# An attention and FFN kernel: T banks taken in turn by all that ScalarE empties, two y banks, projections and the split of batch 0 moved

## What is computed

```python
Q, K, V = (proj(Wq), proj(Wk), proj(Wv))            # einsum('oc,bct->bto', W, x), 16 heads of 8
att = einsum('bhqd,bhkd->bhqk', Q, K) / sqrt(8) + b[0]
att = att * m + (1.0 - m) * NEG_INF                 # m: mask of the keys
y = einsum('bhqk,bhkd->bhqd', softmax(att), V)      # then back to (B, C, T)
h = silu(bit_linear(y, w_gate)) * bit_linear(y, w_up)   # 256 -> 1024
h = rms_norm(h, ln_weight)
out = x + bit_linear(h, w_down)                     # 1024 -> 256
# bit_linear: x rounded to 8 bit by its row maximum, w rounded to -1, 0, 1 by its mean |w|
```

## Time and profile before

| | us |
|---|---|
| median of 3 runs | 220.28 |
| lowest and highest run | 220.03, 223.39 |
| the profiled execution's own time | 221.76 |
| its span in the profile | 220.0 |
| mean granted TensorE clock in it | 0.937 of full speed |

### The profile page before, as it was taken

How to read it: one execution, slowest core, us unless ns; L and a number is a source line. 1 busy time by engine, 2 the same in 40 slices (tenths; PEclk the granted TensorE clock), 3 DMA queues, 4 the chain that set the end, 5 groups by cost and what they waited for, 6 DMA issues and landing times.

```text
span 220.0 us, 4111 instructions
## 1 busy us (share of the span) xinstructions
PE 155.7 (71%) x1378; PEld 69.2 (31%) x1378; DVE 140.9 (64%) x228; ACT 134.3 (61%) x264; POOL 106.5 (48%) x196
## 2 busy tenths in 40 slices
PE   3326859979697697687586587969378758688454
PEld 2222424324333333232242242433122321244243
DVE  5956484865575567557657646646554297699882
ACT  2011115878479588768657636636378757899852
POOL 8329956352317308207302102080873089999960
PEclk9999999997889999999999969587889996999999
DMA  3256712452612461511311210000000000000012
GB/s 123 62 146 211 162 38 55 102 211 73 181 69 53 101 202 46 169 41 36 82 42 45 70 44 2 5 0 2 0 2 3 0 4 3 0 24 24 27 48 72
DMA packets 20068, 14.19 MB, mean 65 GB/s; under 512 B 2112, under 2 KB 19144, under 8 KB 20048
## 3 DMA queue, kind: packets, MB, share of 16 engines
q1 hardware_dynamic: 19184, 13.54, 21.8%
q10 hardware_dynamic: 864, 0.39, 0.7%
HBM read 6.17 MB, written 1.07 MB: 33 GB/s over the span
## 4 chain that ended last, share of the span: by engine, by line
PE 37%; POOL 22%; DVE 14%; issue 13%; ACT 7%; DMA 3%; ACTq 2%; POOLq 1%; SPq 1%; DVEq 0%
PE y_ps L902 14%; PE s_ps L864 8%; DVE maxes L728 8%; POOL hw L418 6%; PE t_ps L881 4%; POOL h_rs L429 3%; PE misc L849 2%; ACT probs L457 2%; PE misc L923 2%; DMA q_st<-nm_rows 2%; ACTq L227 2%; POOL y_q L357 2%; PE misc L840 2%; ACT y_raw L526 2%; DVE y_n L684 1%
## 5 line engine op out<-in xcount | busy, mean ns | idle before, releaser
L728 DVE TENSOR_REDUCE maxes<-s_ps 128x4 f32<-128x1024 f32 x64 | 77.7, 1224 | 53.5 <-PE s_ps L864 53.2
L457 ACT ACTIVATE probs<-t_ps 128x512 f32<-128x512 f32 x128 | 71.2, 595 | 29.9 <-PE t_ps L881 27.0
L864 PE MATMUL s_ps<-k_st,q_st 64*128 64x256 bf16 x256 | 48.3, 315 | 5.7 <-DVE maxes L728 4.0
L902 PE MATMUL y_ps<-probs,v_pad 128*32 128x256 f32 x512 | 46.7, 430 | 5.3 <-ACT y_raw L526 5.2
L881 PE MATMUL t_ps<-q_st,k_st 64*128 64x256 bf16 x256 | 47.2, 300 | 3.2 <-DMA q_st<-nm_rows 1.6
L342 POOL TENSOR_SCALAR nm_parts<-maxes 128x16 bf16<-128x16 f32 x16 | 3.3, 203 | 77.6 <-DVE maxes L728 77.6
L864 PEld LDWEIGHTS s_ps<-k_st,q_st 64*128 64x128 bf16 x256 | 19.1, 102 | 40.2 <-issue 28.3
L418 POOL TENSOR_TENSOR hw<-hid,ln_bc 128x512 f32<-128x512 f32 x16 | 20.0, 1270 | 6.0 <-DVE hid L750 6.0
L983 PE MATMUL s_ps<-w_q,ffn_x 128*128 128x512 bf16 x64 | 17.8, 403 | 6.7 <-DVE hid L750 6.5
L840 PE MATMUL misc<-x_sb,wqk_sb 128*128 128x256 f32 x32 | 14.0, 583 | 10.9 <-ACTq L510 6.6
L881 PEld LDWEIGHTS t_ps<-q_st,k_st 64*128 64x128 bf16 x256 | 17.7, 100 | 12.4 <-ACT probs L457 5.7
(11 more groups left out here) (99 smaller groups left out, 225.4 us busy)
## 6 DMA issues: line engine op xcount, KB each, us to landing
q_st<-parts SPq DMA_DIRECT2D x48, 64.0 KB
k_st<-parts SPq DMA_DIRECT2D x42, 64.0 KB
w_f<-in_wgT SPq DMA_DIRECT2D x1, 1024.0 KB, 5.1
w_f<-in_wuT SPq DMA_DIRECT2D x1, 1024.0 KB, 5.3
w_f<-in_wdT SPq DMA_DIRECT2D x1, 1024.0 KB, 5.9
out<-o_sb SPq DMA_DIRECT2D x8, 128.0 KB, 1.7
x_sb<-in_x SPq DMA_DIRECT2D x1, 512.0 KB, 5.2
mask_bc<-in_cond SPq DMA_DIRECT2D x1, 512.0 KB, 6.5
```

The lines of the kernel that those rows point to most:

```text
L457: act.activation(probs[:, t % NP_RING].rearrange("p e t -> p (e t)"), t_ps[:, t % 2].rearrange("p e t -> p (e t)"), ACT.Exp, scale=SCALE). ...
L728: dve.tensor_reduce(dst[:, :, s, :], s_ps[:, c % 2], AX.X, ALU.max).then_inc(s_maxed, 1)
L864: mm = pe.matmul(s_ps[:, c % 2, i, e, :], q_st[b % 3][rows, hp, qt * P:qt * P + P], k_st[b % 3][rows, hp, :], start=True, stop=True)
L902: last = pe.matmul(y_ps[32 * j:32 * j + 32, tau * T:tau * T + T], v_pad[b % 3][:, kt, h, :], probs[:, (2 * pair + 1 - i) % NP_RING, e, :], ...
```

## The change

- The eight banks of PSUM are cut anew: `misc` is gone, y_ps is two banks, by batch modulo 2. Both transposes of y write into the bank that y came from; the down projection takes these two in turn.
- All else that ScalarE empties (projections of q and k, of V, the transposed maxima, the integers of y, the sum of the weights) takes the two banks of t_ps in turn with the transposed scores. `unit_numbers` lists all of them in order; unit u waits until unit u - 2 is emptied (`give`), and ScalarE counts each one in `unit_free`.
- Rounds run from -1. Batch 0's q and k are projected into s_ps and batches 1, 2 (q, k) and 0 to 2 (V) ahead of the rounds; those of batches 3 to 7 stand in rounds -1 and 0 (QK_SLOTS, V_SLOTS). qk_f has four buffers, v_pad one per batch, with 18 columns per matmul instead of 32.
- Batch 0's parts are split on VectorE without the bias ahead of it; the bias is computed on POOL. SP loads the q parts first, then stores and loads the bias. VectorE clears all stacks.
- POOL's `round_y` is gone: y with the constant is transposed in fp32 and ScalarE subtracts the constant in its copy. y_to_channels stands at k = 6 (before: 7), scale_y at k = 7 (before: 0 of the next round), the integers' transpose at k = 3 (before: 1).
- The x and the mask of batches 3 to 7 are loaded as one group. Weight loads stand ahead of round -1 and in rounds -1 and 0, sums in rounds -1 and 1 (six of 1024 elements instead of twelve of 512), the total in round 2, rounding in rounds 3 to 8, one POOL step each, clipping in rounds 4 to 6.

```diff
-GROUPS = (0, 1, 3, 4, B)
+GROUPS = (0, 1, 3, B)
+HEAD_COLS = 2 * (DH + 1)
+LAG = 1
+FIRST, LAST = -1, B
+QK_SLOTS = {(-1, 0): 3, (-1, 2): 4, (-1, 4): 5, (-1, 7): 6, (0, 7): 7}
+V_SLOTS = {(-1, 1): 3, (-1, 3): 4, (-1, 5): 5, (0, 1): 6, (0, 3): 7}
+WEIGHT_SUM_SLOTS = {(-1, 4): 0, (-1, 5): 1, (-1, 6): 2, (-1, 7): 3, (1, 3): 4, (1, 7): 5}
+WEIGHT_TOTAL_SLOT = (2, 0)
+EARLY = (("qk", 1), ("v", 0), ("qk", 2), ("v", 1), ("v", 2))
...
+def unit_numbers():
+    order = list(EARLY)
+    for n in range(FIRST, LAST + 1):
+        for k in steps(n):
+            pair = 8 * n + k - LAG
+            ongoing = 0 <= pair < 8 * B
+            names = (("t", 2 * pair) if ongoing else None, extra_unit(n, k), ("t", 2 * pair + 1) if ongoing else None)
+            order += [name for name in names if name]
+    order.append(("ints", B - 1))
+    return {name: u for u, name in enumerate(order)}
...
-        y_ps = pb("y_ps", [P, 512], f32)
-        misc = pb("misc", [P, 512], f32)
-        down_ps = [y_ps, misc]
+        y_ps = [pb(f"y_ps{r}", [P, 512], f32) for r in range(2)]
...
@@ sync
-            sp.wait_ge(bias_step, 8)
-            sp.dma_start(bias_scr, bias_parts[:, :, :, :].rearrange("b i k t -> b (i k) t")).then_inc(bias_stored, 16)
-            sp.wait_ge(q_zeroed, 1)
+            load_rows(0)
             load_high(0, 0)
             load_low(0, (0,))
-            load_rows(0)
+            sp.wait_ge(bias_step, 7)
+            sp.dma_start(bias_scr, bias_parts[:, :, :, :].to_broadcast([B, 2, 3, T])).then_inc(bias_stored, 16)
+            load_bias(0)
             load_inputs(2)
-            load_inputs(3)
+            load_weights(0)
...
@@ gpsimd
-            weight_steps = {6: (0, 2), 7: (4, 1, 3, 5)}
+            weight_steps = {3: 0, 4: 2, 5: 4, 6: 1, 7: 3, 8: 5}
+            split_parts(1)
             for n in range(FIRST, LAST + 1):
                 if has(n):
                     negate_maxes(n, 1)
-                if has(n - 2):
-                    round_y(n - 2)
-                if has(n + 3) and n + 3:
+                if has(n + 3):
                     split_parts(n + 3)
...
                 if has(n + 1):
                     negate_maxes(n + 1, 0)
...
@@ scalar
+            def take(name):
+
+                act.wait_ge(unit_ready, unit[name] + 1)
+                return t_bank(unit[name])
...
+            act.wait_ge(qk0_ready, 1)
+            act.activation(qk_f[:, 0, 0, :], s_ps[:, 0, 0, 0, :], ACT.Copy).then_inc(q0_copied, 1)
+            act.wait_ge(k_zeroed, 1)
+            act.wait_ge(hi_ready, 1)
+            load_part(act, 0, 1, 0)
+            copy_qk(1)
+            act.wait_ge(parts_step, 2)
+            load_part(act, 0, 1, 1)
+            act.wait_ge(parts_step, 3)
+            load_part(act, 0, 1, 2)
+            place_values(0)
+            copy_qk(2)
+            place_values(1)
+            place_values(2)
...
@@ vector
+            clear_stacks(0)
+            for r in range(2):
+                dve.memset(y_ps[r][:, :], 0.0).then_inc(y_cleared, 1)
...
             for n in range(FIRST, LAST + 1):
                 for k in steps(n):
-                    if n == 7 and 1 <= k < 7:
-                        clip_weights(*divmod(k - 1, 2))
...
+                    if 4 <= n < 7 and k in (1, 4):
+                        clip_weights(n - 4, k // 4)
+                    if (n, k) == (2, 1):
                         mean_weights()
                     if k == 5 and has(n - 1):
                         normalize_y(n - 1)
-                    if k == 0 and has(n - 2):
-                        scale_y(n - 2)
+                    if k == 7 and has(n - 1):
+                        scale_y(n - 1)
...
@@ tensor
+            def give(name):
+
+                u = unit[name]
+                if u >= 2:
+                    pe.wait_ge(unit_free, u - 1)
+                return t_bank(u)
...
             def project_qk(b):
 
-                take_misc()
+                dst = give(("qk", b))
                 if b in GROUPS:
                     pe.wait_ge(x_in[GROUPS.index(b)], 16)
...
             def values(pair):
...
-                pe.wait_ge(exp_done, 2 * pair + 2)
...
-                    if b:
-                        pe.wait_ge(y_raw_ready, b)
+                pe.wait_ge(unit_free, unit["t", 2 * pair + 1] + 1)
...
+                if w == 0 and b >= 2:
+                    pe.wait_ge(ym_ready, b - 1)
...
+            pe.wait_ge(x_in[0], 16)
+            pe.wait_ge(wqk_in, 16)
+            for side in range(2):
+                pe.matmul(s_ps[:, 0, side, 0, :], wqk_sb[:, side, :], x_sb[:, 0, :], start=True, stop=True)\
+                  .then_inc(qk0_ready, 1)
+            project_qk(1)
+            project_v(0)
+            project_qk(2)
+            project_v(1)
+            project_v(2)
...
-                    if k == 1 and has(n - 2):
+                    if (n, k) in QK_SLOTS:
+                        project_qk(QK_SLOTS[n, k])
+                    if (n, k) in V_SLOTS:
+                        project_v(V_SLOTS[n, k])
+                    if k == 2 and has(n):
+                        transpose_maxes(2 * n + 1)
+                    if k == 3 and has(n - 2):
                         y_ints_to_positions(n - 2)
...
                     if k == 4 and has(n - 1):
                         y_to_positions(n - 1)
...
                     if k == 6 and has(n + 1):
-                        transpose_maxes(n + 1, 0)
-                    if k == 7 and has(n - 1):
+                        transpose_maxes(2 * n + 2)
+                    if k == 6 and has(n - 1):
                         y_to_channels(n - 1)
```

More of the change, by code:

```diff
@@ L85, in adaln_ffn_kernel @@
         q_st = [sb(f"q_st{r}", [P, NHP, T], bf16) for r in range(3)]
-        v_pad = [sb(f"v_pad{r}", [P, QT, NH, 32], f32) for r in range(3)]
+        v_pad = sb("v_pad", [P, B, QT, NHP, PAIR_COLS], f32)
         maxes = sb("maxes", [P, 2, 2, 16], f32)
@@ L210, in adaln_ffn_kernel, with t_bank @@
         o_ready = sem("o_ready")
-        LAG = 1
-        FIRST, LAST = -4, B
-        def steps(n):
-            return range(8 if n < B else 4)
-        def has(b):
-            return 0 <= b < B
+        unit = unit_numbers()
+        def t_bank(u):
+            return t_ps[:, u % 2].rearrange("p e t -> p (e t)")
         def load_part(queue, b, side, part):
@@ L350, in negate_maxes @@
                 pool.tensor_scalar(part[2], r[1], -1.0, 1.0, ALU.mult, ALU.mult).then_inc(nm_step, 1)
[L352 to L361 removed]
+            def split_parts(b):
+                lot, qk = parts[:, b % 2], qk_f[:, b % 4]
+                pool.wait_ge(unit_free, unit["qk", b] + 1)
+                if b in GROUPS:
+                    pool.wait_ge(mask_bc_in[GROUPS.index(b)], 16)
+                pool.tensor_tensor(qk[:, 1, :], qk[:, 1, :], mask_bc[:, b, :], ALU.mult).then_inc(k_masked, 1)
                 pool.wait_ge(k_masked, b + 1)
@@ L905, in values, with transpose_maxes @@
                 last.then_inc(pv_done, 1)
-            def transpose_maxes(b, tau):
-                g = 2 * b + tau
-                take_misc()
+            def transpose_maxes(g):
+                dst = give(("rows", g)).bitcast(bf16)
                 pe.wait_ge(ident_ready, 4)
@@ L1002, in down @@
                     pe.wait_ge(w_ready, 3)
[L1003 to L1005 removed]
+                if b < 2:
+                    pe.wait_ge(ym_ready, B - 1 + b)
                 if b >= 2:
```

388 lines of the change are left out of this document (165 added, 223 removed).

## The result

| | before | changed |
|---|---|---|
| median of four runs | 221.14 us (220.03 to 223.39) | 198.78 us (197.67 to 200.07) |
| ratio to before | | 0.9085 [0.9005, 0.9165] |
| profiled execution, span | 221.76 us, 220.0 | 197.93 us, 196.0 |
| mean granted clock | 0.937 | 0.964 |

A forecast was written before the change was run, and what follows sets the result against it. No engine is full; waiting in a ring costs time. Span 220.0 + 2.4 (front) - 25.1 (rounds 1 to 6) - 0.6 (round 7) - 0.7 (end) = 196.0 us; median 220.28 - 24.0 = 196.3 us, range 188 to 209.

The forecast's parts named there:

- I take 1.3: Rounds 4 to 6: two weight clips of 0.97 us each, partly in VectorE's idle time, add 1.3 us a round.
- The port's bound of 13.5 us: Rounds 4 to 6: if every clip met a 2.90 us VectorE/POOL port wait, 4.5 us more a round, 13.5 in all.
- I take nothing: T banks, three extra units a round from round 1 on: priced at zero, with a bound of 3.6 us a round.
- the rival of half its bound: T ring in rounds 1 to 6: extra units cost 1.8 us a round, giving 207 us; chance 0.12.
- The rival of SP's queue: SP's load issue sets the round, up to 15.5 us in five rounds, giving 204 us; chance 0.14.
- 12.5, just below 13.3: SP's stack-load cycle: 9.0 us to the last part, 2.1 to land, 1.4 to close, against a 13.3 us round.
- 1.35 goes to 0: VectorE's idle 1.35 us a round at the copy of y vanishes, since y_ps is doubled.
- 1.33 - 0.45 us a round: POOL's rounding of y removed: the 1.33 us y_q wait becomes the fp32 transpose itself, 0.45 us.
- 11.16 us and hand-overs: A plain round: VectorE's need of 11.16 us plus 0.45, 0.47, 0.56, 0.3 and 0.35, making 13.3 instead of 16.62.
- I take 1.00: TensorE's granted clock in rounds 1 to 6 taken as 1.00; where it stayed 0.74, 1 to 2 us a round return.
- x in time: Front: x arrives in time or TensorE warms at once, first maximum at 15.8, front 6 us shorter, 190 us; chance 0.09.
- Slower than before: T ring exceeds its bound: at 0.6 us for each of 40 extra units the gain is gone, at 0.75 226 us; chance 0.05.

The follow-up runs named there:

- the clips' run: The changed kernel with the weight clips moved to round 7, POOL's three last roundings after them: 200.54 us, 0.9032 of the kernel before.
- the four-stack run: The changed kernel with four buffers of k_st and q_st instead of three: 196.04 us, 0.8887 of the kernel before.
- one more unit: The changed kernel with a spare unit (two transposes, one unread ScalarE copy) on the T banks in each of rounds 1 to 7: 199.36 us, 0.9053.
- the yardstick: The changed kernel unaltered, timed again in the first group of follow-up runs: 199.74 us, 0.9074 of the kernel before.
- the early load: The changed kernel with x of batches 3 to 7 loaded right behind wv instead of behind the bias: 196.97 us, 0.8952 of the kernel before.

## Why the prediction was right, and where it was not

The time: 196.3 us forecast, 198.78 measured, in the range and in the direction given. The span was forecast at 196.0 and is 196.0, which is luck: the terms were not all right.

*Rounds 1 to 6*: 84.4 forecast, 84.48 measured, by errors that cancel. Singly 14.0, 13.3, 13.3, 14.6, 14.6, 14.6 were forecast, and 14.34, 14.13, 16.17, 13.47, 13.46, 12.91 came.
- "I take 1.3" for two clips was wrong by all or nearly all of it, by the clips' run and the four-stack run together. Their 0.97 us was a mean too, of one that took 2.38 beside POOL's long operation and five of about 0.7; alone a clip is 0.68. The step that failed is that VectorE's maxima "set the pace" wherever TensorE is not held; at 12.0 of 13.46 us VectorE has room, and the loads of the stacks lie on the chain. Rounds 4 to 6 were so forecast 1.1, 1.1 and 1.7 us too long. The port's bound of 13.5 us was far off for clips that stand apart, but the mechanism is real: in a row they cost 1.6 us of round 6.
- "I take nothing" for the T ring was too little, by the price of one more unit: 0.3 us as a mean, 0.25 to 0.68 in rounds 4 to 6. If the three units that the kernel has cost as much, an estimate and not measured, that is 0.8 to 2.0 us a round, about the rival of half its bound (1.8); the clips' 1.3 was not there beside it.
- The rival of SP's queue was given 0.14. It was partly true: 1.8 us at equal clock and up to 3.0, most of it in round 3. "12.5, just below 13.3" was too short: from one reuse of a stack to the next, 93.48 to 107.93, the loop took 14.45 us, of which 9.38 to the last part (9.0 in the prediction), 3.68 until it landed (2.1) and 1.39 to the close (1.4). By the prediction's own sign of being wrong, a wait on the stack loads above 1 us a round, the sum was wrong in rounds 2 and 3 (1.65 and 2.60 us).
- That the waits of misc and y_q end was right, and the y_q wait is what mattered most: 12.7 of the 25.0 us return with POOL's rounding alone, 6.0 with the projections. No run brings back the whole of round 6 (8.8 us): POOL's rounding returns 3.3 of it and the clips in a row 1.6; the two together were not tried. That "1.35 goes to 0" was right; that the second bank does it was wrong (0.1 us). The forecast priced it at 1.33 - 0.45 us a round. In the new ring it is worth 2.4 to 3.3, with TensorE and ScalarE stopping together and a lower clock (0.81 to 0.91 in these rounds); the sum held because the round was built up from 11.16 us and hand-overs, not from these prices.
- The clock: "I take 1.00" held for five rounds of six in this profile, and not in each execution: round 1 took 14.34 and 15.56 us at 1.00 and 0.89, and 17.21 at 0.80 with the integers at k = 1. The median's 2.5 us above the forecast are not in the span, which is as forecast: the execution of before stood 1.5 above its median, and that was carried over, while this one stands 0.85 below its own.

*The front*: +2.4 forecast, +1.0 measured (+1.8 in the yardstick). The mechanism was right (the first maximum waits for x: 22.5 forecast, 21.11 measured, and TensorE waits 2.57 us for it), the transfer was mis-sized: 4.5 us to land, not 6.0. That "x in time" would bring 6 us was wrong: the early load brings 0.6 to 1.4, since the rows of the bias are late instead. With no projection in front of the first scores the first maximum did come at 15.87 us, as "15.8" said, and the first copy only 3.3 us earlier.

*Round 7* -0.6 and -0.7. *The end*: -0.7 forecast, +0.7 measured, at a granted clock of 0.89; in the other profiles this stretch took between 47.96 and 49.94 us without any edit to it, so the term is below what can be told.

*Slower than before* needed 0.6 us at all 40 units; 0.3 was measured as a mean. Its point of decision was the right one.

Of what would show it, round 3 at 13.3 us with idles under 0.6 was wrong (16.17, idle 2.03) and nearly right for rounds 4 and 5 (13.47, but with two clips in them, and one idle of 0.81 in the timeline of VectorE in round 5):

```profile
112.85 1.23 DVE L712 TENSOR_REDUCE maxes<-s_ps 128x4 f32<-128x1024 f32 x1 [0.81 <-PE s_ps L845]
...
118.01 1.22 DVE L712 TENSOR_REDUCE maxes<-s_ps 128x4 f32<-128x1024 f32 x1 [0.28 <-PE s_ps L845]
...
121.29 1.23 DVE L712 TENSOR_REDUCE maxes<-s_ps 128x4 f32<-128x1024 f32 x1 [0.22 <-PE s_ps L845]
```

What sets the 13.46 us of these rounds stays open. No engine is full (TensorE 11.60, VectorE 12.02, ScalarE 10.47 us). With three stacks the loads are on the chain of both; with four they are gone from that of round 5, and the round is as long. Taking 1.15 us from VectorE did nothing, and adding 0.65 us of ring (0.28 TensorE, 0.37 ScalarE) added 0.25 to 0.68. This speaks for TensorE and ScalarE taking turns through the two T tiles as the path behind the loads; a third T tile was not tried.

## What to carry to other kernels

An operation on a third engine, between two engines of a ring, can cost more than its time. It waits in that engine's own line (here behind five operations on a maximum), and it stops whatever shares the ring: 2.4 to 3.3 us for a rounding of 0.40 us. When a stall is taken out, look at the path with the least slack, the loads' issue too; one more buffer made the rounds 1.8 us shorter at equal clock. A step that a busy engine shares is not priced by that engine's idle time; take work out of it and see whether the round follows, and if it doesn't, check that no other path of the same length held it. Keep VectorE's long element-wise work away from the moment at which POOL's small operations are waited for. And take a second profile of the same kernel before reading a difference of a few tenths.
